# Latent inputs of batches 1 to 7 made inside the perceiver, context worked first

## The chip, the cores and the metric

One NeuronCore of one Trainium2 chip runs the whole program. The metric is the device time of one execution in microseconds (us); lower is better. TensorE is the matrix engine, VectorE, ScalarE and GpSimd are the elementwise engines, and SP (SyncE) mostly issues DMAs.

## The reference, cut to what matters

Two layers over x (8 batches, 512 tokens, D = 512) with a context of 77 rows a batch. The part that matters here is the hand-over from layer 0 to the cross attention of layer 1:

```
out0 = einsum(alpha, slot_values) @ wo + bo          # layer 0's slot feed-forward
x2   = x1 + out0                                     # residual
xn   = layernorm(x2);  z  = layernorm(xn) * ln_l_g + ln_l_b     # the latents of layer 1
cn   = layernorm(ctx); zc = cn * ln_x_g + ln_x_b
q    = z @ Wq                                        # 16 heads of 64
k, v = concat(z, zc) @ Wkv                           # 512 + 77 keys
o    = softmax(q k' / 8, masked) v                   # per batch and head
```

The two nested norms of x2 are worked as one (the variance v becomes v (1 + eps) + eps squared). Behind it come Wout, a norm and a routed expert feed-forward on x2. Every product with a weight is made of a high and a low float32r part (three products for one), to keep float32 accuracy.

## The kernel before, in words

The program is a row of stages, each a block of instructions with its own buffers, queues and semaphores, and a barrier between two stages: `build_layer0` (0 to 676 us), `build_slots` (to 828), `build_latents` (to 1000), `build_perceiver` (to about 2485) and `build_experts`. Each engine's program is written out by hand in order, and every dependence is an explicit wait on a semaphore mark.

**Slots** (lines 999 to 1322) makes vo_s, the slots' values already multiplied by wo. It also splits the weights Wq and Wkv through three staging areas of WihT; when the last is cut, SP loads x1 of batches 0 and 1 into two of these areas (line 1100), where the next stage finds them.

**Latents** (lines 1325 to 1651) runs over the 8 batches. For each, TensorE makes the read-out alpha @ vo (`read_out`, line 1478, 4 tiles of 128 tokens; a last row of ones with bo gives the bias); VectorE adds x1 (line 1608), measures it (1611, 1616), GpSimd makes the root (1466, 1468), VectorE normalises (1631), TensorE transposes (1486), ScalarE scales by the gains (1556) and casts the high part (1560), VectorE takes the low part (1641), and x2 and both parts of z go to HBM. Beside them the stage works the context rows once: statistics (1594), normalising (1623), transposes (1495, 1500), scaling and cast (1537 to 1546), low part (1638). Then, one head pair of keys per batch (`keys`) and ten value units of 128 rows x 512 columns spread over the batches (`values`), it makes the context's keys and values for all heads and stores them (Kc_s, Vc_s). Keys and values share banks 6 and 7, and the value tile in SBUF is single, so the cast of a tile waits for the store of the tile before. The context rows themselves are loaded by SP at this stage's start (line 1428) behind the first small loads, ahead of the gains.

**Perceiver** (lines 1661 to 2131) runs over 128 heads (8 batches x 16) in 512 steps of one tile of 128 queries, four steps to a head and eight to a pair of heads. In step n TensorE issues the scores of step n + 1 into one of two score banks, then, by n modulo 4: the last two products with the values of the head before last (0), transposes of two of the five key blocks of probabilities (1), transposes of two more and two products (2), the last transposes and a product (3). Once per pair it also makes the query (n = 1 modulo 8) and the key (3) of the next pair, and in steps 6 and 7 a value unit. VectorE takes the minimum of the negated scores of step n (line 2113), the reciprocals (2109) and all low parts (2066, 2081, 2098); ScalarE the exponentials (2034), all high parts (2005) and the output's cast (2053); GpSimd multiplies the probabilities (1880) and takes the output's low part (1874). Queries, keys, values and transposes share three banks: `claim` gives a unit the bank that was released longest ago and waits until VectorE has read the unit that lay there before. SP, in one program per pair, loads the context's keys and values, copies halves, loads z at each batch's last pair, stores the output two pairs late, and clears a part of the experts' buffer.

Of the kernel before, what the change touches and what calls it, by code (L numbers as in the profile page):

```python
# [20 lines left out]
P = 128  # L21
# [90 lines left out]
def f32(ap):  # L112

    return ap.bitcast(F32)
# [884 lines left out]
def build_slots(nc, orders, a, si_s, vo_s, Wq, Wkv, Wout_s, gh_s, WihT, x1_s):  # L999
# [11 lines left out]
    with ExitStack() as ctx:  # L1011
# [71 lines left out]
        def _(sp):  # L1083
# [15 lines left out]
            for n in range(2):  # L1099
                sp.dma_start(stage(n), x1_s[n:n + 1].rearrange("b (t p) d -> p (b t) d", p=P)).then_inc(x1_in, 16)  # L1100
# [5 lines left out]
            sp.wait_ge(x1_in, 32)  # L1106
# [218 lines left out]
def build_latents(nc, orders, a, x1_s, alphaT_s, vo_s, x2_s, z_s, Kc_s, Vc_s, Wkv, ahead):  # L1325
# [13 lines left out]
    RING = 3  # L1339

    with ExitStack() as ctx:
# [18 lines left out]
        rows_c = [f32(z_hi[1][:, k, :]) for k in range(KT - 1)] + [f32(z_lo[1][0:LAST, 0, :])]  # L1360
# [3 lines left out]
        setup, small, ones_row, cx_in = sem("setup"), sem("small"), sem("ones_row"), sem("cx_in")  # L1364
        x1_in = [sem(f"x1_in{r}") for r in range(RING)]
# [10 lines left out]
        batch = lambda b: 0 <= b < B  # L1376
        v_items = [(k, h) for k in range(KT) for h in range(2)]
        v_of = lambda b: v_items[b * len(v_items) // B:(b + 1) * len(v_items) // B]
        place = {"x2": lambda b, t: (b * NT + t) % 3, "zT": lambda b, c: 3 + (b * C + c) % 3, "cT": lambda c: 3 + c % 3,
# [20 lines left out]
        def _(sp):  # L1400
            flat = a["ctx_1024"].rearrange("b s d -> (b s) d")
            def load_small(b):
                m = b % 2
                if b >= 2:
                    sp.wait_ge(*pe_s.after("x2", b - 2, NT - 1))
# [3 lines left out]
            def load_x(b):  # L1409
                r = b % RING  # L1410
                if b >= RING:
                    sp.wait_ge(x2_out[r], 16 * (b // RING))
                    sp.wait_ge(*dve_s.after("xn", b - RING, NT - 1))
                sp.dma_start(X[r], x1_s[b:b + 1].rearrange("b (t p) d -> p (b t) d", p=P)).then_inc(x1_in[r], 16)
# [12 lines left out]
            for k in range(KT):  # L1427
                sp.dma_start(rows_c[k], flat[k * P:k * P + rows_of(k), :]).then_inc(cx_in, 16)
            for dst, src in smalls:
                sp.dma_start(dst, src).then_inc(small, 16)  # L1430
            load_small(1)
            load_x(2)
            for b in range(B):
                sp.wait_ge(*dve_s.after("free", "x2", b, NT - 1))
                sp.dma_start(x2_s[b:b + 1].rearrange("b (t p) d -> p (b t) d", p=P), X[b % RING]).then_inc(x2_out[b % RING], 16)
                if batch(b + 2):
                    load_small(b + 2)
                if batch(b - 1):
                    for q, h in [i for i in v_of(b - 1) if i[1]]:
                        values_out(q)  # L1440
                    keys_out(b - 1)
                if batch(b + 2) and b > 0:
                    load_x(b + 2)
# [1462 lines left out]
```

## Time and profile before

| what | us |
| --- | --- |
| median of 3 runs (2917.95 to 2927.77) | 2923.05 |
| the profiled execution | 2921.61 |
| its span | 2919.8 |
| TensorE busy in it | 2646.1 (91%) |
| VectorE, ScalarE, GpSimd busy | 2023.6, 1517.6, 1522.0 |
| mean granted TensorE clock | 0.953 of full |

The profile is of one execution; its times are microseconds from the span's start. In the names, la_ is a buffer of the latents stage, pa_ of the perceiver, sl_ of slots, ex_ of the experts. "128x512 fp32r<-128x512 f32 x4" says what an instruction writes, from what, and how many stand in the group; PEld is the weight load, SPq and ACTq are DMA issues on those engines' queues; "[0.31 <-DVE pa_PTl L2066]" says how long the engine was idle before the instruction and what ended that. A granted clock of 1.00 is 2.4 GHz, one of 0.50 is 1.2 GHz. A row of the view of stretches gives start:end, length, and the busy time (with the number of instructions) of TensorE, its weight loads, VectorE, ScalarE and GpSimd, then the granted clock, the share of the DMA engines and GB/s.

### The profile page before, as it was taken

How to read it: one execution, taken by the hardware profiler on the slowest of the kernel's cores; microseconds unless marked ns; L12 is line 12 of the kernel's file. 1: busy time of each engine (PE TensorE's matmuls, PEld its weight loads, DVE VectorE, ACT ScalarE, POOL GpSimd, SP SyncE). 2: the span in 40 equal slices, each digit the busy share in tenths (PEclk: the TensorE clock that was granted, in tenths of full speed). 3: DMA queues.
4: the chain of work that ended last, by engine and by line, in shares of the span. 5: the costliest groups of instructions: out<-in, count | busy, mean ns of one | idle time of the engine just before them, and what ended most of it. 6: DMA issues, size and time to landing. Idle time of an engine off the chain costs nothing. (4 is left out here: it accounts for less than half of the span.)

```text
span 2919.8 us, 41005 instructions
## 1 busy us (share of the span) xinstructions
PE 2646.1 (91%) x14566; PEld 2188.7 (75%) x14566; DVE 2023.6 (69%) x4005; ACT 1517.6 (52%) x2897; POOL 1522.0 (52%) x1149
## 2 busy tenths in 40 slices
PE   6699999986778699999999999999999998799698
PEld 5577777763436588888888888888888887677476
DVE  3677777742546377777777777777777777577666
ACT  2234334331213277777777777777777777111175
POOL 2355544320000166666666666666666666465555
PEclk9899999998878899999999999999999999899899
DMA  5212222133348633334333343233433314668475
GB/s 188 56 54 56 56 57 57 41 96 128 139 145 312 228 74 80 106 83 115 81 77 109 80 118 81 75 111 76 122 80 77 109 51 136 210 238 288 157 275 187
DMA packets 212526, 351.15 MB, mean 120 GB/s; under 512 B 75839, under 2 KB 82370, under 8 KB 204631
## 3 DMA queue, kind: packets, MB, share of 16 engines
q1 hardware_dynamic: 193539, 284.89, 32.8%
q0 software_dynamic: 11680, 45.02, 4.2%
q10 hardware_dynamic: 7104, 18.61, 1.6%
q8 instruction: 117, 1.92, 0.3%
q14 instruction: 86, 0.70, 0.1%
HBM read 172.47 MB, written 156.64 MB: 113 GB/s over the span
## 5 line engine op out<-in xcount | busy, mean ns | idle before, releaser
L1880 POOL TENSOR_SCALAR pa_Pr<-pa_Pr,pa_rs 128x590 f32<-128x590 f32 x512 | 902.4, 1769 | 485.1 <-DVE pa_rs L2109 484.9
L2113 DVE TENSOR_REDUCE pa_least<-pa_S 128x1 f32<-128x590 f32 x512 | 390.7, 763 | 230.0 <-PE pa_S L1944 227.9
L2034 ACT ACTIVATE pa_Pr<-pa_S,pa_least 128x590 f32<-128x590 f32 x512 | 385.5, 753 | 99.4 <-DVE pa_least L2113 96.0
L2066 DVE TENSOR_TENSOR pa_PTl<-pa_W,pa_PTh 128x512 fp32r<-128x512 f32 (+1 forms) x640 | 421.2, 684 | 20.5 <-ACT pa_PTh L2005 16.4
L2005 ACT ACTIVATE pa_PTh<-pa_W 128x512 fp32r<-128x512 f32 (+1 forms) x640 | 367.0, 596 | 58.4 <-PE pa_W L1955 47.1
L1955 PE MATMUL pa_W<-pa_ident,pa_Pr 128*128 128x128 f32 (+1 forms) x2560 | 369.7, 275 | 0.6
L1955 PEld LDWEIGHTS pa_W<-pa_ident,pa_Pr 128*128 128x128 f32 (+1 forms) x2560 | 302.4, 142 | 30.0 <-POOL pa_Pr L1880 2.8
L1971 PE MATMUL pa_O<-pa_PTh,pa_V 128*128 128x512 f32 (+1 forms) x640 | 289.2, 452 | 18.6 <-DVE pa_PTl L2066 14.4
L1972 PE MATMUL pa_O<-pa_PTl,pa_V 128*128 128x512 f32 (+1 forms) x640 | 253.4, 396 | 0.0
L1942 PE MATMUL pa_S<-pa_U,pa_Qh 128*128 128x296 f32 (+1 forms) x1024 | 228.9, 305 | 7.5 <-ACT pa_Pr L2034 0.5
L1942 PEld LDWEIGHTS pa_S<-pa_U,pa_Qh 128*128 128x128 f32 x1024 | 183.2, 188 | 55.5 <-ACT pa_Pr L2034 21.3
L1944 PE MATMUL pa_S<-pa_Um,pa_Ql 128*128 128x296 f32 (+1 forms) x1024 | 222.7, 299 | 0.0
L514 POOL TENSOR_TENSOR l_E<-l_E,l_rs 128x1232 f32<-128x1232 f32 x32 | 81.1, 2533 | 204.0 <-DVE l_rs L916 204.0
L1944 PEld LDWEIGHTS pa_S<-pa_Um,pa_Ql 128*128 128x128 f32 x1024 | 166.4, 189 | 0.0
L1971 PEld LDWEIGHTS pa_O<-pa_PTh,pa_V 128*128 128x128 f32 (+1 forms) x640 | 121.4, 190 | 45.0 <-DVE pa_PTl L2066 36.1
L119 PE MATMUL pa_W<-Wkv_hi,pa_z_hi 128*128 128x256 f32 x512 | 144.9, 283 | 0.0
L120 PE MATMUL pa_W<-Wkv_lo,pa_z_hi 128*128 128x256 f32 x512 | 144.2, 282 | 0.0
L121 PE MATMUL pa_W<-Wkv_hi,pa_z_lo 128*128 128x256 f32 x512 | 143.9, 281 | 0.0
L1972 PEld LDWEIGHTS pa_O<-pa_PTl,pa_V 128*128 128x128 f32 (+1 forms) x640 | 123.0, 192 | 5.2
L2560 ACT ACTIVATE ex_xT_hi<-ex_bank 128x512 fp32r<-128x512 f32 x92 | 53.4, 599 | 141.3 <-PE ex_bank L2456 134.9
L119 PE MATMUL pa_W<-pa_z_hi,Wq_hi 128*128 128x512 f32 x256 | 106.9, 418 | 17.8 <-POOL pa_Ql L1871 17.8
L2005 ACT ACTIVATE pa_U<-pa_W 64x512 fp32r<-64x512 f32 x128 | 75.8, 592 | 89.7 <-PE pa_W L121 88.1
(503 smaller groups left out, 6545.6 us busy)
## 6 DMA issues: line engine op xcount, KB each, us to landing
xs_s<-pa_Ql SPq DMA_DIRECT2D x57, 576.0 KB
pa_Um<-pa_U SPq DMA_DIRECT2D x128, 147.5 KB
pa_Qh<-pa_Qh SPq DMA_DIRECT2D x128, 128.0 KB
o_s<-pa_O_hi SPq DMA_DIRECT2D x64, 256.0 KB, 2.0
o_s<-pa_O_lo SPq DMA_DIRECT2D x64, 256.0 KB, 2.3
Wkv_hi<-o_s SPq DMA_DIRECT2D x8, 2048.0 KB, 11.3
Wkv_lo<-o_s SPq DMA_DIRECT2D x8, 2048.0 KB, 17.0
l_xa<-x SPq DMA_DIRECT2D x8, 1024.0 KB, 6.5
```

The lines of the kernel that those rows point to most:

```text
L119: pe.matmul(out, a[0], b[0], start=first, stop=False)
L120: pe.matmul(out, a[0], b[1], start=False, stop=False)
L1880: pool.tensor_scalar(p, p, rs[:, g % 2, t:t + 1], None, ALU.mult).then_inc(*pool_s.mark("probs", n))
L1942: pe.matmul(out[:, a0:a1], qh, U[p % 2][x][:, a0:a1], start=True, stop=False)
L1944: m = pe.matmul(out[:, a0:a1], ql, Um[p % 2][x][:, a0:a1], start=False, stop=True)
L1955: m = pe.transpose(bank_of[u][0:KEYS[c], t * P:(t + 1) * P], Pr[g % 2][:, t, c * P:c * P + KEYS[c]], ident[:, :])
L1971: pe.matmul(Oc[:, :], v, PTh[0:n, r, :], start=(c == 0), stop=False)
L1972: pe.matmul(Oc[:, :], v, PTl[0:n, r, :], start=False, stop=(c == NC - 1)).then_inc(*pe_s.mark("PV", g, c))
L2005: act.activation(out, src, ACT.Copy, scale=scale).then_inc(*act_s.mark("hi", *name))
L2034: act.activation(Pr[g % 2][:, t, :], scored[n % 2], ACT.Exp, scale=-1.0, bias=least[:, g % 2, t:t + 1], accum_out=rs[:, g % 2, t:t + 1]).t ...
L2066: dve.tensor_tensor(out, src, f32(hi_ap), ALU.subtract).then_inc(*dve_s.mark(*name))
L2113: dve.tensor_reduce(least[:, g % 2, t:t + 1], scored[n % 2], AX, ALU.min).then_inc(*dve_s.mark("least", n))
```

## The change

The latents stage keeps only batch 0 of the latents (FIRST = 1). Context rows come with the slots stage's last loads (in the place of batch 1's x1) and are worked first: TensorE transposes them ahead of the read-out, VectorE takes their low parts ahead of batch 0's adding. The eight key pairs and ten value units follow in a loop of their own, with batch 0's transposes, casts and low parts behind the first pair.

The latents of batches 1 to 7 are made in the perceiver, one tile of 128 tokens at a time, 28 tiles, in the steps of the batch before. Tile t of batch b starts in step n0 = 64 (b - 1) + 12 t, and its parts are put at fixed distances: inputs fetched at n0 - 2 (ScalarE's DMA queue), ones row n0 - 1 (VectorE), read-out n0 (TensorE), add and measure n0 + 1 (VectorE), root n0 + 2 (GpSimd) and x2 stored (ScalarE's queue), normalise n0 + 3 (VectorE), transpose n0 + 4 (TensorE), scale n0 + 5 (VectorE, where it was ScalarE), cast n0 + 6 (ScalarE), first store n0 + 7 and low part (VectorE), second store n0 + 8. To make room in SBUF, the output's sum and its low part share one buffer: ScalarE's first write of a pair's output waits for the store of the pair before, the output's cast on ScalarE and low part on GpSimd come one step earlier (t = 1 in place of 2).

```diff
@@ build_slots, SP
-            for n in range(2):
-                sp.dma_start(stage(n), x1_s[n:n + 1].rearrange("b (t p) d -> p (b t) d", p=P)).then_inc(x1_in, 16)
+            sp.dma_start(stage(0), x1_s[0:1].rearrange("b (t p) d -> p (b t) d", p=P)).then_inc(x1_in, 16)
+            sp.dma_start(stage(1)[:, 0:whole, :], flat[0:whole * P, :].rearrange("(k p) d -> p k d", p=P)).then_inc(x1_in, 16)
+            sp.dma_start(stage(2)[0:flat.shape[0] - whole * P, 0, :], flat[whole * P:, :]).then_inc(x1_in, 16)
@@ build_latents
-    RING = 3
+    RING, FIRST = 1, 1
@@ TensorE
             pe.wait_ge(setup, 4)
+            context()
             pe.wait_ge(ones_row, 2)
             pe.wait_ge(small, 16 * len(smalls))
-            read_out(0)
-            context()
-            for b in range(B):
-                if batch(b + 1):
-                    read_out(b + 1)
-                transposed(b)
+            for b in range(FIRST):
+                read_out(b)
+            for b in range(PAIRS):
                 keys(b)
                 for k, h in v_of(b):
                     values(k, h)
+                if batch(b):
+                    transposed(b)
@@ build_perceiver
+        APART = 3 * NT
+        tiles = [(b, t) for b in range(1, B) for t in range(NT)]
+        begins = {STEPS // B * (b - 1) + APART * t: i for i, (b, t) in enumerate(tiles)}
+        tile_at = lambda n, late: begins.get(n - late)
@@ SP
             def load(b):
+                if b:
+                    sp.wait_ge(z_out, 32 * NT * b)
@@ GpSimd
-                if t == 2 and g >= 3 and g % 2 == 1:
+                if t == 1 and g >= 3 and g % 2 == 1:
                     low_part((g - 3) // 2)
+                i = tile_at(n, 2)
+                if i is not None:
+                    pool.wait_ge(*dve_s.after("x2 var", i))
+                    pool.tensor_scalar(lve, lmv[:, 1:2], 1.0 + EPS, EPS * EPS, ALU.mult, ALU.add).then_inc(*pool_s.mark("x2 ve", i))
+                    pool.wait_ge(*pool_s.after("x2 ve", i))
+                    pool.tensor_tensor(lrstd, lve, minus_half, ALU.pow).then_inc(*pool_s.mark("x2 rstd", i))
@@ TensorE
+            def residual(i):
+                u = ("x2", i)
+                claim(u)
+                pe.wait_ge(x_in, 32 * (i + 1))
+                pe.wait_ge(vo_in, 16 * (i // NT + 2))
+                pe.wait_ge(*dve_s.after("ones", i))
+                pe.matmul(bank_of[u][:, :], alphas[0:NS + 1, :], vo[:, :], start=True, stop=True).then_inc(*pe_s.mark(*u))
+                release(u)
+            def latent(i):
+                u = ("zT", i)
+                claim(u)
+                pe.wait_ge(*dve_s.after("xn", i))
+                for c in range(C):
+                    m = pe.transpose(bank_of[u][:, c * P:(c + 1) * P], ln[:, c * P:(c + 1) * P], ident[:, :])
+                m.then_inc(*pe_s.mark(*u))
+                release(u)
@@ ScalarE
+            def fetch(i):
+                ...
+                    act.wait_ge(z_out, 32 * i)
+                act.dma_start(lx[:, :], x1_s[b, t * P:(t + 1) * P, :]).then_inc(x_in, 16)
+                act.dma_start(alphas[0:NS, :], alphaT_s[b][:, t * P:(t + 1) * P]).then_inc(x_in, 16)
+                ...
                     if x == 0 and p > 0:
-                        act.wait_ge(*pool_s.after("O lo", p - 1))
+                        act.wait_ge(o_out, 32 * p)
@@ VectorE
+            def add_and_measure(i):
+                dve.wait_ge(*pe_s.after("x2", i))
+                dve.tensor_tensor(lx[:, :], bank_of["x2", i][:, :], lx[:, :], ALU.add).then_inc(*dve_s.mark("read", "x2", i))
+                ...
+            def normalised(i):
+                dve.wait_ge(*pool_s.after("x2 rstd", i))
+                dve.wait_ge(*dve_s.after("x2 var", i))
+                dve.tensor_scalar(ln[:, :], lx[:, :], lmv[:, 0:1], lrstd, ALU.subtract, ALU.mult).then_inc(*dve_s.mark("xn", i))
+            def scaled(i):
+                ...
+                for c in range(C):
+                    m = dve.tensor_scalar(ln[:, c * P:(c + 1) * P], bank_of["zT", i][:, c * P:(c + 1) * P], gain[0][:, c:c + 1], gain[1][:, c:c + 1],
+                                          ALU.mult, ALU.add)
+                m.then_inc(*dve_s.mark("read", "zT", i))
+            def latent_low(i):
+                dve.wait_ge(*act_s.after("z hi", i))
+                dve.tensor_tensor(ln[:, :], ln[:, :], lx[:, :], ALU.subtract).then_inc(*dve_s.mark("z lo", i))
@@
+                for late, work in ((-1, ones), (1, add_and_measure), (3, normalised), (5, scaled), (7, latent_low)):
+                    if tile_at(n, late) is not None:
+                        work(tile_at(n, late))
```

## Rows read from the trace of the kernel before

**Rows 1.** View of stretches: the latents stage, and the perceiver's steps.
```profile
828.40:999.70 171.30, 124.57 (x524) 90.96 (x524) 100.09 (x207) 59.45 (x102) 14.05 (x22) 0.82 0.72 263
...
1018.80:2467.00 1448.20, 1427.38 (x8856) 1254.68 (x8855) 1122.38 (x2097) 1051.21 (x2157) 975.33 (x572) 1.00 0.34 93
```

**Rows 2.** Timeline of VectorE at the latents' start: start us, us, instruction.
```profile
828.72 1.02 DVE L1589 MEMSET la_aT<- 1x512 f32 x2 [2.55 <-PEq L1011]
836.86 2.47 DVE L1594 BATCH_NORM_STATS2 la_cstats<-la_z_hi 128x6 f32<-128x512 f32 x4 [7.11 <-DMA la_z_lo<-ctx]
...
839.96 0.45 DVE L1598 BATCH_NORM_AGGREGATE la_cmv<-la_cstats 128x2 f32<-128x6 f32 x5
...
848.42 1.88 DVE L1623 TENSOR_SCALAR la_z_hi<-la_z_hi,la_cmv,la_crstd 128x512 f32<-128x512 f32 x4
```

**Rows 3.** Timeline of TensorE, the same stretch.
```profile
848.99 4.41 PE L1495 MATMUL la_bank<-la_ident,la_z_hi 128*128 128x128 f32 x16 [4.01 <-DVE la_z_hi L1623]
...
853.73 3.62 PE L1478 MATMUL la_bank<-la_vo,la_aT 65*128 65x512 f32 x8
857.18 1.48 PE L1486 MATMUL la_bank<-la_ident,la_xn 128*128 128x128 f32 x12
...
861.60 0.41 PE L119 MATMUL la_bank<-la_zc_hi,Wkv_hi 128*128 128x308 f32 x1 [2.13 <-DVE la_zc_lo L1638]
```

**Rows 4.** Timeline of GpSimd, the same stretch.
```profile
849.07 1.27 POOL L1468 TENSOR_TENSOR la_rstd<-la_ve,la_minus_half 128x4 f32<-128x4 f32 x1
```

**Rows 5.** Timeline of ScalarE: cast of the context, a DMA issue.
```profile
856.79 1.31 ACT L1546 ACTIVATE la_zc_hi<-la_K_lo 128x616 fp32r<-128x616 f32 x2
...
966.80 0.33 ACTq L1562 DMA_DIRECT2D z_s<-la_z_hi  x1
```

**Rows 6.** Timeline of TensorE: two value units, first and last of 24.
```profile
983.84 0.48 PE L119 MATMUL la_bank<-Wkv_hi,la_zc_hi 128*104 128x512 f32 x1 [0.73 <-DVE la_K_lo L1646]
...
989.25 0.39 PE L121 MATMUL la_bank<-Wkv_hi,la_zc_lo 128*104 128x512 f32 x1
```

**Rows 7.** Timeline of TensorE in one head pair of the perceiver.
```profile
1314.87 0.47 PE L119 MATMUL pa_W<-pa_z_hi,Wq_hi 128*128 128x512 f32 x1
...
1330.04 0.66 PE L1955 MATMUL pa_W<-pa_ident,pa_Pr 128*128 128x128 f32 x4
...
1335.81 0.40 PE L1971 MATMUL pa_O<-pa_PTh,pa_V 77*128 77x512 f32 x1
```

**Rows 8.** Timeline of VectorE and GpSimd in the slots stage.
```profile
774.40 0.89 DVE L1237 COPY sl_AT<-sl_bank 128x128 f32<-128x128 f32 x4
...
778.62 0.69 DVE L1300 TENSOR_TENSOR sl_y<-sl_bank,sl_bv_bc 128x512 f32<-128x512 f32 x1 [2.20 <-PE sl_bank L1172]
...
780.08 0.18 DVE L1304 BATCH_NORM_AGGREGATE sl_mv<-sl_stats 128x2 f32<-128x6 f32 x1
...
782.83 1.19 DVE L1251 TENSOR_TENSOR Wkv_lo<-WihT,Wkv_hi 128x1024 fp32r<-128x1024 f32 x1
...
783.01 1.10 POOL L1117 TENSOR_SCALAR sl_rstd<-sl_mv 128x1 f32<-128x1 f32 x1 [0.88 <-DVE sl_mv L1304]
...
788.32 0.44 POOL L1117 TENSOR_SCALAR sl_rstd<-sl_mv 128x1 f32<-128x1 f32 x1 [0.90 <-DVE sl_mv L1304]
```

**Rows 9.** Timeline of VectorE in the same head pair as rows 7.
```profile
1327.69 0.69 DVE L2098 TENSOR_TENSOR pa_O_sum<-pa_O,pa_O_sum 64x512 f32<-64x512 f32 x1
...
1329.31 1.28 DVE L2066 TENSOR_TENSOR pa_PTl<-pa_W,pa_PTh 128x512 fp32r<-128x512 f32 x2
...
1333.76 0.68 DVE L2066 TENSOR_TENSOR pa_PTl<-pa_W,pa_PTh 77x512 fp32r<-77x512 f32 x1
```

**Rows 10.** Timeline of GpSimd in that pair.
```profile
1328.68 1.77 POOL L1880 TENSOR_SCALAR pa_Pr<-pa_Pr,pa_rs 128x590 f32<-128x590 f32 x1 [3.10 <-DVE pa_rs L2109]
...
1332.48 1.28 POOL L1874 TENSOR_TENSOR pa_O_lo<-pa_O_sum,pa_O_hi 128x512 fp32r<-128x512 f32 x1
```

**Rows 11.** DMA issues on the page; the last number is us from issue to landing.
```profile
o_s<-pa_O_lo SPq DMA_DIRECT2D x64, 256.0 KB, 2.3
```

More of the change, by code:

```diff
@@ L1566, in low_out @@
                 act.dma_start(z_s[1][b], f32(z_lo[b % 2][:, :, :])).then_inc(z_out[b % 2], 16)
-            for b in range(B):
-                latents(b)
+            for b in range(PAIRS):
                 for h in range(2):
@@ L1582, in _ @@
                     act.activation(hi, src, ACT.Copy).then_inc(*act_s.mark("hi", "V", k, h))
-            for m in range(2):
-                act.wait_ge(z_out[m], 32 * (B // 2))
+                if batch(b):
+                    latents(b)
+                if batch(b - 1):
+                    low_out(b - 1)
+            act.wait_ge(z_out[0], 32)
         @block.vector
@@ L1632, in _, with low @@
                                       ALU.subtract, ALU.mult).then_inc(*dve_s.mark("xn", b, t))
[L1633 to L1638 removed]
+            def low(b):
+                m = b % 2
                 for c in range(C):
@@ L1641, in _ @@
                     dve.tensor_tensor(z_lo[m][:, c, :], full[m][:, c, :], f32(z_hi[m][:, c, :]), ALU.subtract).then_inc(*dve_s.mark("lo", b, c))
+            add_and_measure(0)
+            normalised(0)
+            for b in range(PAIRS):
                 for h in range(2):
@@ L2000, in _ @@
                     value(q, j)
+                if tile_at(n, 0) is not None:
+                    residual(tile_at(n, 0))
+                if tile_at(n, 4) is not None:
+                    latent(tile_at(n, 4))
         @block.scalar
@@ L2057, in _ @@
                     probabilities(g - 1, 4)
+                if tile_at(n, -2) is not None:
+                    fetch(tile_at(n, -2))
+                if tile_at(n, 2) is not None:
+                    keep(tile_at(n, 2))
+                i = tile_at(n, 6)
+                if i is not None:
+                    act.wait_ge(x2_out, 16 * (i + 1))
+                    act.wait_ge(*dve_s.after("read", "zT", i))
+                    act.activation(l_hi, ln[:, :], ACT.Copy).then_inc(*act_s.mark("z hi", i))
+                i = tile_at(n, 7)
+                if i is not None:
+                    act.wait_ge(*act_s.after("z hi", i))
+                    latent_out(0, i)
+                i = tile_at(n, 8)
+                if i is not None:
+                    act.wait_ge(*dve_s.after("z lo", i))
+                    latent_out(1, i)
                 if STEPS <= n < STEPS + 4:
```

151 lines of the change are left out of this document (81 added, 70 removed).

## The prediction

> **What bounds the kernel now.** I read the view of stretches first. The latents stage (828.4 to 999.7) takes 171.3 us, in which TensorE is busy 124.6 us at a granted clock of 0.82; the 1448.2 us of the perceiver's steps show TensorE busy 1427.4 us at clock 1.00, VectorE 1122.4, ScalarE 1051.2, GpSimd 975.3 [rows 1]. So the first stage is a chain of waits, and the second is TensorE's: 64 head pairs of 22.6 us, eight steps each. Work moved from one to the other leaves a stage where it partly hid and enters one where every TensorE microsecond counts. Then I read the timelines of the latents' start and of one head pair (1313 to 1337).
>
> **The latents stage: its start.** Before, VectorE's context statistics wait for the context rows until 836.86, though its own work would let them start at 829.8 (two memsets end at 829.74) [rows 2]. In the new stage they start there. Statistics and aggregates take 3.55 us (836.86 to 840.41), GpSimd's root 1.8 us (what it took for batch 0, from the aggregates' end at 848.51 to 850.34) [rows 2, 4]; then the normalised rows. TensorE's first transpose comes 0.57 us after their start (848.42 to 848.99) [rows 2, 3]: 829.8 + 3.55 + 1.8 + 0.6 = 835.7. Transposes and four read-out products took TensorE 8.4 us (848.99 to 857.35), so it would be at 844.1 [rows 3]. ScalarE's cast of the context ends 9.1 us after the first transpose (848.99 to 858.10) [rows 3, 5]: 844.8. Keys start about 844, 17.6 us sooner than at 861.60 [rows 3]. The new loads in the slots stage (1.2 MB of context in place of 1 MB of x1) go out behind the last weight cut, on SP, some 30 us before that stage ends: nothing.
>
> **Its body.** 24 value products of 512 columns take 5.65 us (983.84 to the last start, 989.25, and one spacing), so 2.83 us per value unit; key pairs of 24 products with 308 columns 3.4 us, by columns [rows 6]. Eight key pairs and ten value units: 55.5 us. They share banks 6 and 7, and a bank is free only when ScalarE and VectorE have read it, some 1.4 us. In the new order VectorE does batch 0's adding, measuring and normalising (5.6 for four of the 1.64 below less its gaps, 1.8 for the root, 1.9 for four normalisings [rows 8, 4, 2]) after the context's low parts (845.6) and ahead of the first key's low part, so value (0,0) starts about 855.6 instead of 847.5. It ends 858.4, the latents' transposes about 861.5, key pair 1 at 865; value (0,1) waits until 866.7 for a bank, behind the latents' casts on ScalarE and low parts on VectorE. Left are nine value units and six key pairs, 45.9 us, five bank waits of 1.2 to 1.5 us, and one of 5 us where value (2,0) follows value (1,1) directly and ScalarE needs the store of the whole first tile landed: 11.6 us. With 4 us for stretches at the lower clock TensorE ends at 928; the end took 10.2 us (989.5 to 999.7), now 9.7 as the keys' stores go first. New end 937.7: **62 us less**, with bounds of 52 (clock 0.82 all through, a second store wait) and 66 (no low clock).
>
> **The perceiver: plain costs.** For each of 28 tiles TensorE gets a read-out product, 0.86 us (four in 3.45 us from 853.73 to 857.18, the next group's first row), and four transposes, 0.40 us (twelve took 1.48 with the last one's drain) [rows 3]: 1.26 us, 35 in all. VectorE gets add, statistics and aggregate, 1.64 us (778.62 to 780.26) [rows 8]; normalising 0.5 (four in 1.88, 848.42) [rows 2]; scaling four blocks, 0.9 (the nearest row copies four 128x128 blocks in 0.89) to 1.1, taken 1.0 [rows 8]; a low part 0.65 (two in 1.28) [rows 9]; a memset, under 0.5 (two of 1x512 took 1.02) [rows 2]: 4 to 4.3 us, some 115 in all, against 326 us idle [rows 1]. ScalarE gets a cast (0.6; two of 616 columns took 1.31) and five or six DMA issues of 0.33 us, 0.43 with the gap [rows 5]; GpSimd 0.9 to 1.8 us. None of these three becomes the bound as a sum. They matter where a bank is claimed: TensorE has three banks, takes the longest released, and waits for VectorE's last read of it.
>
> **The perceiver: waits.** I replay one pair with the new work in its places; steps are counted modulo 8. In the trace VectorE runs without a gap from the scores' minimum of step 5 through the key's low parts and the output sum (from 1327.69, end 1328.38) to the first low part of the probabilities (1329.31 to 1329.95), and TensorE's third transpose group, which needs that bank, starts at 1330.04: in steps 5 and 6 any VectorE time delays TensorE one for one [rows 9, 7].
> Tiles 0 and 2 (start in step 0): the product costs 0.86. VectorE's 1.64 fall in idle time behind the query's 2.8 us. In step 4 come the transposes; in step 5 VectorE scales behind the output sum, and the value unit of step 6 draws exactly this bank: TensorE moves by the scaling, 1.0, in place of 0.4. Sum 1.9 us.
> Tiles 1 and 3 (start in step 4): the product's 0.86 is inside VectorE's 1.64, which sits in the gapless run: 1.6 us. GpSimd then gets its factor 1.7 us late, at 1330.2, does the probabilities (1.77), the pair's low part (1.28), which the change puts one step earlier, the next probabilities (1.77), and only then the variance and root, 0.9 [rows 10]: ready at 1336.1. VectorE reaches the normalising at 1334.5 and waits 1.6. The fifth low part (1333.76 to 1334.44) ends at 1338.4; the product on it (1335.81) starts there, 2.6 late [rows 9, 7]. Then 0.4 for the transposes, and the query draws their bank: scaled at 1342.2. The query starts 4.6 us late against 1314.87 plus the pair. Sum 4.6.
> 14 tiles of each: **91 us**. At the start tile 0's inputs are issued on ScalarE about 1018.5 and land behind other loads; TensorE would wait for them some 2.5 us. The earlier reuse of the output sum, which now waits for its store, costs nothing while GpSimd ends it in step 6 and stores land in 2.3 us [rows 11]; without that, up to 1 us on ScalarE per pair. SP gains a wait ahead of each latents load, in front of a pair's store and its blanks; the last part of a batch goes out seven steps before, so it holds nothing up. ScalarE's fetch waits for the store of the tile before, with the exponentials behind it; that store goes out two steps (5 us) sooner, and 256 KB landed in 2.3 us [rows 11]: nothing either.
>
> **A rule against the trace.** One GpSimd scalar operation on 128x1 took 1.10 us (783.01) while VectorE ran a subtraction of two SBUF operands (782.83 to 784.02) [rows 8]; the same operation took 0.44 us at 788.32, with no such subtraction beside it [rows 8]. The Trainium skill, "SBUF — State Buffer", section "Who interferes with whom", says that such a VectorE instruction and a GpSimd one that reads SBUF exclude each other, the later waiting for the whole of the earlier. By that rule each tile's new low part would wait for GpSimd's 1.77 us. The sum above leaves this out; it is part of rival D.
>
> **Sum.** The profiled execution took 2921.61 us, its span 2919.8, the median of three 2923.05. 2921.6 - 62 + 2.5 + 91 = 2953.1, so **2953 us** (the median is 1.4 above its base).
>
> **Rivals.**
> A, the forecast: bank waits and the late root add to the moved work. For it: the gapless run [rows 9]. Against: one pair was replayed, and the bank order by hand. 0.43.
> B, the moved work is hidden but for TensorE's own time: 2921.6 - 62 + 2.5 + 35 = 2897, up to 2905 with short waits. For it: three engines have over 300 us idle each [rows 1]. Against: the gapless run sits in the very steps used. This is the case on the other side; it decides for faster if waits per tile stay under 0.55 us, (62 - 2.5 - 35 - 9) / 28. 0.24.
> C, bank waits as in A, but the root is not late (tiles 1 and 3 cost 2.8): 14 x (1.9 + 2.8) = 66, 2928. 0.18.
> D, A plus inputs of a tile that land after TensorE asks for them (256 KB took 2.3 us alone [rows 11], the fetch goes out 4 us ahead into SP's store and blanks, 0 to 1.5 us on 28 tiles) or VectorE waiting for GpSimd, 0 to 0.8 us a tile: up to 42 + 22 us on top, 2970 to 3015. 0.12.
> E, the latents stage is bound by the bank pair and its stores throughout, and saves only 50 with C's costs: 2940. 0.03.
>
> **Numbers.** A measurement of this kernel can tell about 0.3% (9 us) from no change. Faster by more: B, 0.24. Within: most of C, 0.17. Slower: A, D, E and the rest of C, 0.59. The range, 2898 to 2990, takes in B at its middle and D's lower half.
>
> **What would show it.** The latents stage 105 to 120 us long, its first statistics near 829.8, keys near 844; 4.6 us lost on odd tiles and 1.9 on even ones; steps from 1448 to some 1540 us; VectorE's normalising waiting on GpSimd's root; TensorE waiting on the scaling. The forecast is wrong if a batch with tiles is less than 8 us longer than before (then B or C), or if the latents stage saves less than 50.

## The result, and the profile after

The changed kernel takes 2962.87 us (median of 4 runs, 2962.23 to 2965.04) against 2923.64 (4 runs of the kernel before on the same chip): ratio 1.0137, 95% interval 1.0119 to 1.0155. It is slower. The profiled execution took 2963.48 us, its span is 2961.7.

First the two stretches of [rows 1] in the kernel after: the latents stage, and the steps of the perceiver.

```profile
833.00:939.00 106.00, 72.16 (x356) 59.06 (x356) 33.57 (x67) 24.37 (x46) 3.46 (x10) 0.87 0.34 128
958.10:2512.50 1554.40, 1476.23 (x9016) 1273.32 (x9016) 1222.33 (x2373) 1069.01 (x2182) 995.13 (x628) 0.99 0.40 107
```

The latents stage took 171.3 us and takes 106; the steps took 1448.2 and take 1554.4, with TensorE busy for 1476.2 of them, VectorE for 1222.3. TensorE's idle time in this stretch rose from 21 us to 78, of which 13.5 is one stall near its end (below).

For the accounting both traces are divided at instructions that both have: VectorE's first memset of the latents stage, the first exponential of step 0, that of step 504 (eight steps from the end), that of step 511, the end. The kernel before, then after:

```profile
828.70:1020.30 191.60, 137.45 (x596) 102.39 (x597) 104.83 (x215) 62.42 (x107) 21.19 (x42) 0.81 0.70 253
1020.30:2454.00 1433.70, 1413.88 (x8772) 1243.48 (x8771) 1110.26 (x2073) 1040.66 (x2134) 962.79 (x565) 1.00 0.34 90
2454.00:2471.10 17.10, 13.60 (x84) 10.85 (x82) 12.25 (x26) 11.95 (x26) 14.99 (x10) 1.00 0.82 304
2471.10:2919.80 448.70, 382.61 (x1818) 304.24 (x1818) 292.13 (x653) 140.51 (x225) 242.97 (x350) 0.90 0.63 222
```

```profile
833.30:960.50 127.20, 85.90 (x435) 71.38 (x436) 38.48 (x76) 27.34 (x51) 10.38 (x29) 0.85 0.38 135
960.50:2487.30 1526.80, 1462.26 (x8933) 1261.28 (x8932) 1211.79 (x2351) 1059.87 (x2162) 984.66 (x622) 1.00 0.39 105
2487.30:2515.60 28.30, 14.23 (x82) 11.81 (x81) 12.47 (x25) 12.03 (x26) 13.57 (x9) 0.76 0.49 183
2515.60:2961.70 446.10, 379.19 (x1822) 300.01 (x1820) 293.67 (x653) 139.98 (x225) 244.31 (x350) 0.91 0.63 223
```

The second number of a row is its length. Differences: 64.4 us less up to step 0; 93.1 more in steps 0 to 504; **11.2 more in the last eight steps**; 2.6 less behind them; and 4.6 us more ahead of the first mark, in code that is the same but for the loads (over the traces of this study that mark falls anywhere from 826.2 to 834.3, so experiments are read by stretch). Together 41.9, the difference of the spans. In steps 0 to 504 TensorE's busy time rose by 48.4 us and its idle time by 44.7.

The start of the latents on TensorE, against [rows 3]:

```profile
840.32 4.17 PE L1476 MATMUL la_bank<-la_ident,WihT 128*128 128x128 f32 x16 [10.32 <-DVE WihT L1595]
...
844.68 3.62 PE L1459 MATMUL la_bank<-la_vo,la_aT 65*128 65x512 f32 x8
848.25 0.41 PE L119 MATMUL la_bank<-la_zc_hi,Wkv_hi 128*128 128x308 f32 x1
...
859.30 0.79 PE L119 MATMUL la_bank<-Wkv_hi,la_zc_hi 128*128 128x512 f32 x1 [6.53 <-DVE la_K_lo L1621]
```

Keys begin 15.0 us after the memset at 833.3, where they took 32.9 (forecast 844 - 828.7 = 15.3). Then a hole of 6.5 us opens ahead of the first value unit: VectorE reaches the key's low part only behind batch 0's adding, measuring and normalising. That was forecast (first value unit 26.9 us after the memset, measured 26.0).

What the steps wait for (engine, line, what released it: us in total, times, longest):

```profile
PE pa_W L119 <- DVE pa_xn_next L2197: 26.0, 28, 1.0
...
DVE pa_xn_next L2191 <- POOL pa_norm L1884: 22.0, 14, 1.6
ACT pa_O_sum L2029 <- DMA o_s<-pa_O_sum: 20.8, 6, 13.9
...
PE pa_S L1944 <- ACT pa_Pr L2084: 13.6, 2, 13.5
...
PE pa_W L1982 <- DMA pa_vo<-vo_s: 5.0, 4, 2.4
```

L2191 is the normalising: it waits for GpSimd's root 14 times, up to 1.6 us, just the odd tiles. L2197 is the scaling: TensorE waits for its bank 28 times. The longest wait for value vectors, 2.4 us, is the first tile's (2.5 was forecast). L2029 is ScalarE's first copy into a pair's output sum: one of its waits is 13.9 us, and TensorE's scores stand still for 13.5 with it. The clock granted in that stretch is 0.76 instead of 1.00.

One odd tile (its step 0 at 1193), VectorE and then GpSimd, against [rows 9, 10]:

```profile
1200.27 0.69 DVE L2134 TENSOR_TENSOR pa_PTl<-pa_W,pa_PTh 128x512 fp32r<-128x512 f32 x1
1201.18 0.69 DVE L2134 TENSOR_TENSOR pa_PTl<-pa_W,pa_PTh 128x512 fp32r<-128x512 f32 x1 [0.21 <-ACT pa_PTh L2029]
1203.44 0.55 DVE L2191 TENSOR_SCALAR pa_xn_next<-pa_x_next,pa_norm 128x512 f32<-128x512 f32 x1 [1.57 <-POOL pa_norm L1884]
```

```profile
1199.45 1.27 POOL L1870 TENSOR_TENSOR pa_O_sum<-pa_O_sum,pa_O_hi 128x512 f32<-128x512 f32 x1
1200.71 1.77 POOL L1876 TENSOR_SCALAR pa_Pr<-pa_Pr,pa_rs 128x590 f32<-128x590 f32 x1
1202.56 0.19 POOL L1882 TENSOR_SCALAR pa_norm<-pa_norm 128x1 f32<-128x1 f32 x1
1202.83 0.57 POOL L1884 TENSOR_TENSOR pa_norm<-pa_norm 128x1 f32<-128x1 f32 x1
```

GpSimd does probabilities, the pair's low part, probabilities, and only then the root, which ends at 1203.40; VectorE had been free since 1201.87. From the starts of the exponentials, twelve steps from a tile's step 0 against the same steps before: an odd tile costs 3.86 us (mean of 14, 3.6 to 4.8), an even one 2.53 (mean of 13), and the very first 6.3. A batch's last 16 steps cost nothing.

### The profile page after: what moved, and what is told of

The parts are those of the page before. It is cut to its first block and busy times, and to the rows that moved or that the text cites. A ratio compares the mean times of both kernels' runs of the same rounds, so it can differ in the third digit from the quotient of the medians.

```text
span 2961.7 us, 41403 instructions
## 1 busy us (share of the span) xinstructions
PE 2645.0 (89%) x14566; PEld 2174.4 (73%) x14566; DVE 2060.3 (70%) x4145; ACT 1501.8 (51%) x2869; POOL 1533.0 (52%) x1192
## 5 line engine op out<-in xcount | busy, mean ns | idle before, releaser
L2029 ACT ACTIVATE pa_PTh<-pa_W 128x512 fp32r<-128x512 f32 (+1 forms) x640 | 368.8, 596 | 88.4 <-PE pa_W L1957 78.7
L1957 PEld LDWEIGHTS pa_W<-pa_ident,pa_Pr 128*128 128x128 f32 (+1 forms) x2560 | 302.7, 142 | 40.1 <-DVE pa_PTl L2134 10.9
L1944 PE MATMUL pa_S<-pa_U,pa_Qh 128*128 128x296 f32 (+1 forms) x1024 | 242.4, 318 | 17.3 <-ACT pa_Pr L2084 13.6
L2209 DVE RECIPROCAL pa_rs<-pa_rs 128x1 f32<-128x1 f32 x512 | 80.8, 158 | 64.9 <-ACT pa_Pr L2084 62.4
```

The lines of the kernel that those rows point to most:

```text
L1944: pe.matmul(out[:, a0:a1], qh, U[p % 2][x][:, a0:a1], start=True, stop=False)
L1957: m = pe.transpose(bank_of[u][0:KEYS[c], t * P:(t + 1) * P], Pr[g % 2][:, t, c * P:c * P + KEYS[c]], ident[:, :])
L2029: act.activation(out, src, ACT.Copy, scale=scale).then_inc(*act_s.mark("hi", *name))
```

## The experiments

Totals are medians; a ratio is to runs of the kernel before on the same chip. "Steps" means steps 0 to 504 of the profiled execution, 1433.7 us before and 1526.8 in the changed kernel. How far one such reading can be trusted: four kernels that leave these steps without tiles (share_only, ctx_first, ctx_keys, norm_ahead) show 1433.2 to 1434.2, but store_first, whose instructions are the changed kernel's up to step 504, shows 1532.8, 6.0 more. With tiles, a difference of a few us in the steps is read from the cost of the single tiles.

### 1. What a tile costs, engine by engine

**TensorE alone** (te_only). Latents for all eight batches ahead of the perceiver (that stage is experiment 4's first), the changed kernel's shared output buffer with its earlier cast and low part, and of the tiles only this:

```diff
 def residual(i): / def latent(i):
-    pe.wait_ge(x_in, ...); pe.wait_ge(vo_in, ...); pe.wait_ge(*dve_s.after("ones", i))
-    pe.matmul(bank_of[u], alphas[0:NS + 1, :], vo)
+    pe.matmul(bank_of[u], ident[0:NS + 1, :], vo)
-    m = pe.transpose(bank_of[u][...], ln[...], ident)
+    m = pe.transpose(bank_of[u][...], ident, ident)
+def freed(kind, i):                      # VectorE
+    dve.wait_ge(*pe_s.after(kind, i))
+    dve.tensor_copy(lve, bank_of[kind, i][:, 0:1])
```

> Latents stage as in the run with the context first, with all eight batches; in the perceiver's steps 28 tiles of TensorE's work alone: a read-out product and four transposes of constant tiles, each bank freed by a copy of one column by VectorE; no fetch, no sum, no statistics, no root, no scaling, no store. The output is complete. Theory (TensorE is busy 1426 of 1446 us, so its own work costs its full time): 28 x 1.26 = 35 us more than the run with the context first alone, steps about 1481 us. Rival (part of it falls into waits that TensorE has anyway, or the third bank decides): 15 to 25 us, or over 45 us.

Measured 2960.18 us, ratio 1.0136 (1.0114 to 1.0158). The two rows are steps 0 to 504 and the last eight:

```profile
1019.80:2479.50 1459.70, 1441.74 (x8939) 1261.89 (x8938) 1115.19 (x2128) 1044.51 (x2135) 961.96 (x566) 1.00 0.34 88
2479.50:2508.20 28.70, 14.48 (x82) 12.06 (x81) 12.41 (x25) 11.97 (x26) 13.49 (x9) 0.76 0.48 180
```

Steps 1459.7 us, 25.7 more than the 1434.0 of the run with the context first: 0.92 us a tile, not 1.26 (two one-column copies on VectorE included). That is 9 us under the theory and just above the rival's 15 to 25. TensorE is busy 27.6 us more (1441.7 against 1414.1), a fifth less than the 35 forecast. The clock is not the reason: the rows that gave 1.26 stand in a stretch (853.7 to 857.3) with a granted clock of 1.00, and a read-out product takes 0.59 us there as here. Where the rest went is not shown. The last eight steps took 28.7 us though no tile falls into them: the tiles do not make this stall, and the shared buffer is in this kernel too (experiment 3).

**VectorE's and ScalarE's part on top** (te_dve, te_act). The same with VectorE's operations of a tile on constant data, without root, rounding, fetch or store; and with ScalarE's fetches, rounding and stores on data that nobody reads:

```diff
-for late, work in ((1, lambda i: freed("x2", i)), (5, lambda i: freed("zT", i))):
+for late, work in ((-1, ones), (1, add_and_measure), (3, normalised), (5, scaled), (7, latent_low)):
```

> The run with TensorE's tile work alone, and with it VectorE's operations of a tile (memset, sum, statistics, aggregation, normalising, four scalings, low part) on constant tiles: no root on GpSimd, no rounding, no fetch and no store on ScalarE. Output complete. Steps 0 to 504 took 1459.7 us with TensorE's work alone and 1526.8 us in the changed kernel; 10.5 of these 67 us were the root's order. Theory (VectorE's 4.6 us a tile, 28 times, lie in the loop of scores, minimum and exponential that sets a step): 40 to 57 us more, 1500 to 1517 us. Rival (ScalarE's queue with its five issues of DMAs and one rounding a tile is what is left): at most 20 us more, under 1480 us.

> The run with TensorE's tile work alone, and with it ScalarE's part of a tile: the fetches, the store of the sum, the rounding and the two stores of the halves, with data that nobody reads, into rows of the batch before that are no longer needed. Output complete. Theory (VectorE holds most of the 67 us): 5 to 15 us over the 1459.7 us of steps 0 to 504. Rival (ScalarE's issues, 0.33 to 0.54 us each, stand between two exponentials): 35 us or more, 1495 us or more.

Measured 3010.98 us, ratio 1.0301 (1.0278 to 1.0324), and 2971.55 us, ratio 1.0178 (1.0153 to 1.0203). The latents stage of these two is not the changed kernel's, so only the steps count:

```profile
1028.70:2535.00 1506.30, 1456.07 (x8939) 1262.79 (x8938) 1217.66 (x2351) 1047.51 (x2135) 964.08 (x566) 1.00 0.33 86
```

```profile
1023.80:2490.60 1466.80, 1445.48 (x8933) 1263.16 (x8932) 1114.89 (x2128) 1056.27 (x2163) 963.50 (x566) 1.00 0.41 109
```

VectorE adds 46.6 us, ScalarE 7.1. Both came as expected. Half of the 7.1 is the very first tile, whose inputs land late (5.0 us in that run against 1.5 without the fetch). With TensorE's 25.7 and the 10.6 of the root (next) that makes 90.0 of the 93.1 us. By tile, te_dve costs 2.39 us an even tile and 2.69 an odd one, against 2.53 and 3.86 in the changed kernel: even tiles are TensorE's and VectorE's work and little else, odd ones have the root on top. VectorE does 102.5 us more work there than with TensorE's part alone (1217.7 against 1115.2): a little under half of it shows in the time.

### 2. The waits inside a tile

**The root ahead of the probabilities** (root_early).

```diff
 for n in range(STEPS):
     g, t = divmod(n, NT)
+    (the four lines that wait for "x2 var" and make the root)
     pool.wait_ge(*dve_s.after("rsum", n))
     ...
-    (the same four lines)
```

> The changed kernel, but GpSimd makes a tile's root ahead of that step's probabilities instead of behind them. Theory (VectorE's 1.57 us wait on the root, 14 times in tiles that start in step 4 mod 8, is on the path): odd tiles fall from 3.85 to about 2.4 us, 14 x 1.4 = 20 us, total about 2943 us. Rival (VectorE's wait was hidden, and what lengthens odd tiles is the order of banks): the wait is gone from the trace but the total stays within 3 us of 2963. Third way (probabilities late by .76 us hold up the transposes): some 5 to 10 us only.

Measured 2955.67 us, ratio 1.0114 (1.0092 to 1.0137). Steps 1516.2, 10.6 less; odd tiles from 3.86 to 2.87 us, even ones nearly unchanged (2.53 and 2.64). The theory, 20 us, missed by half; the total, 7 us lower, lies where the third way had it, though its reason is not shown. The wait is gone, but part of its place is taken by a longer normalising (durations ns min/median/max):

```profile
L2191 DVE TENSOR_SCALAR pa_xn_next<-pa_x_next,pa_norm x28: 536/718/911, 973.9 to 2248.1; 128x512 f32<-128x512 f32 x28
L2203 DVE TENSOR_TENSOR pa_xn_next<-pa_xn_next,pa_x_next x28: 680/682/684, 984.3 to 2261.3; 128x512 f32<-128x512 f32 x28
```

```profile
1201.22 0.57 POOL L1879 TENSOR_TENSOR pa_norm<-pa_norm 128x1 f32<-128x1 f32 x1
1201.78 5.26 POOL L1882 TENSOR_SCALAR pa_Pr<-pa_Pr,pa_rs 128x590 f32<-128x590 f32 x3
```

```profile
1201.92 0.89 DVE L2191 TENSOR_SCALAR pa_xn_next<-pa_x_next,pa_norm 128x512 f32<-128x512 f32 x1
```

In odd tiles it now runs beside GpSimd's probabilities and takes 0.89 us instead of 0.55. 1.57 - 0.35 would be 1.2 us a tile; 1.0 came. The other 0.2 is not explained.

**The scaling in two operations** (scale_two).

```diff
-for c in range(C):
-    m = dve.tensor_scalar(ln[block c], bank[block c], gain[0][:, c:c + 1], gain[1][:, c:c + 1], ALU.mult, ALU.add)
-m.then_inc("read zT")
+dve.tensor_tensor(rows(ln), rows(bank), wide[0], ALU.mult).then_inc("read zT")
+dve.tensor_tensor(rows(ln), rows(ln), wide[1], ALU.add).then_inc("z full")
```

ScalarE's cast then waits for "z full".

> The changed kernel, but the scaling is one product with the broadcast gain, which frees the bank, and one sum with the broadcast offset in SBUF, about 0.69 and 0.65 us in place of four operations of 0.40. Theory (TensorE's 26 us of waits for the scaling, 28 times, are on the path and fall by about 0.8 us each): 15 to 22 us less, 2941 to 2948 us. Rival (VectorE's time as such is what a tile costs, and that falls by 0.2 us a tile): 2957 to 2960 us.

Measured 2959.55 us, ratio 1.0122 (1.0096 to 1.0148); steps 1519.5, 7.3 less. From 1060 to 2440 us, weight loads (PEld) and matmuls of TensorE:

```profile
PEld pa_W L119 <- DVE pa_xn_next L2198: 12.9, 25, 0.6
...
PE pa_W L1957 <- DVE pa_PTl L2134: 12.1, 25, 0.6
```

In the changed kernel the first of these was 29.8 us, 25 times; so the wait for the scaled bank fell by more than half, 17 us. But the second was 7.5 us, 13 times: transposes of the probabilities now wait more often for VectorE's next pieces. A bank freed earlier moves part of the wait to what VectorE does after it. The total is the rival's (2957 to 2960), the theory's 15 to 22 us did not come. But the rival's reason is not shown either: by it every tile falls by 0.2 us, and what fell is the odd tiles alone, from 3.86 to 3.21 (mean of 14), while the even ones stayed (2.53 and 2.63).

**All tiles in one phase** (phase_even).

```diff
-begins = {STEPS // B * (b - 1) + APART * t: i ...}
+begins = {STEPS // B * (b - 1) + (APART * t if b == 1 else 4 * NT * t - 2 * NT): i ...}
```

> The changed kernel with the tiles of batches 2 to 7 started in steps -8, 8, 24 and 40 of the batch before instead of 0, 12, 24 and 36, so that all of them start in step 0 mod 8 (batch 1's stay). Theory (a tile that starts in step 4 mod 8 costs 3.85 us, one in step 0 mod 8 costs 2.45 us): 12 tiles x 1.4 = 17 us less, 2944 to 2949 us. Rival (the tile at -8 meets the four value units at the end of a batch, three banks for all of them, and loses the gain): 2955 us or more.

Measured 2977.72 us, ratio 1.0179 (1.0153 to 1.0205): 15 us slower than the changed kernel, steps 1537.7, 10.9 more. A batch's first 48 steps fell by 3 to 6 us; about 2.5 of that is the tile that moved out of them, the rest is near the theory's 1.4 each for the tiles at 8 and 40. But the tile at -8 cost 5 to 8 us in a batch's last eight steps. From 1060 to 2440 us:

```profile
PEld pa_W L1982 <- issue: 16.1, 10, 4.3
...
PE pa_W L1982 <- DMA pa_vo<-vo_s: 12.3, 6, 3.8
```

Its read-out product waited for the batch's value vectors, up to 3.8 us, in the steps where four value units share three banks. The rival was right, and named only half of it: I had not priced the load.

### 3. The stall in step 504

**The shared output buffer alone** (share_only), on the kernel before:

```diff
-O = sb("O_sum", [P, T])
-Os = pair("O", [P, T])
+Os = sb("O_hi", [P, T], F32R), sb("O_sum", [P, T])
+O = Os[1]
...
-act.wait_ge(*pool_s.after("O lo", p - 1))
+act.wait_ge(o_out, 32 * p)
```

> The kernel before with one part of the change alone: the low part of a pair's output is written over the sum, so ScalarE's first copy of a pair waits for the store of the pair before, and the rounding and the low part come a step earlier. Theory (this part alone makes the stall of 13 us in step 504, of which 3 to 6 us come back after the last scores): 7 to 11 us over before, all of it in the last eight steps. Rival (the stall needs the late steps of the changed kernel): no difference to before.

Measured 2937.03 us, ratio 1.0042 (1.0021 to 1.0063).

```profile
1022.40:2455.60 1433.20, 1413.04 (x8771) 1243.39 (x8771) 1109.24 (x2072) 1042.58 (x2134) 962.55 (x566) 1.00 0.34 90
2455.60:2485.50 29.90, 14.72 (x83) 12.33 (x82) 12.53 (x26) 12.06 (x27) 13.64 (x9) 0.77 0.47 177
```

The steps take what they took before (1433.2), the last eight 29.9 instead of 17.1: 12.8 us, by this part of the change alone. Behind them the experts' first product comes 1.2 us sooner after step 511 than before. The forecast priced it at nothing.

**The store first** (store_first), on the changed kernel:

```diff
-if p == PAIRS - 1:
-    ahead()
 if p >= 2:
     store(p - 2)
+if p == PAIRS - 1:
+    ahead()
```

> The changed kernel, but in the last pair SyncE stores pair 61's output before it issues the loads ahead for the experts. Theory (the 13.9 us stall of ScalarE in step 504 is the store queued behind the 1 MB weight load, and the shared output buffer made it bind): the stall goes, the last eight steps lose 11 us, of which some 3 to 5 us come back after the last scores because the loads start two steps later; total 2952 to 2959 us. Rival (the weight load is needed just as early): the same wait turns up at its split in steps 512 to 515 and the total stays at 2963.

Measured 2956.82 us, ratio 1.0111 (1.0085 to 1.0138). SyncE's issues in the changed kernel, and then with the store first:

```profile
2480.55 0.53 SPq L1780 DMA_DIRECT2D Wq_lo<-Wout_s  x1
...
2481.86 3.68 SPq L1783 DMA_DIRECT2D Wkv_lo<-o_s  x1
2485.59 6.39 SPq L1775 DMA_DIRECT2D o_s<-pa_O_hi  x1
2492.02 0.55 SPq L1775 DMA_DIRECT2D o_s<-pa_O_sum  x1
```

```profile
2489.31 0.33 SPq L1775 DMA_DIRECT2D o_s<-pa_O_hi  x1
...
2490.22 0.41 SPq L1780 DMA_DIRECT2D Wq_lo<-Wout_s  x1
...
2491.39 5.71 SPq L1783 DMA_DIRECT2D Wkv_lo<-o_s  x1
```

```profile
958.30:2491.10 1532.80, 1465.51 (x8932) 1263.75 (x8931) 1212.23 (x2351) 1059.19 (x2162) 984.47 (x622) 1.00 0.39 104
2491.10:2505.40 14.30, 13.10 (x82) 10.64 (x81) 12.37 (x25) 11.89 (x26) 13.53 (x9) 1.00 0.99 350
2505.40:2959.20 453.80, 382.93 (x1822) 304.43 (x1820) 289.46 (x653) 140.45 (x225) 243.37 (x350) 0.90 0.63 222
```

In the changed kernel the store of pair 61 is issued behind 6 MB of loads for the experts (three of 2 MB; the theory named one of 1 MB), the issue alone takes 6.4 us, and ScalarE's copy that waits for it starts at 2502.08. With the store first the last eight steps take 14.3 us, 14.0 less. The stretch behind them is 7.7 us longer. Of these, 5.8 lie between step 511 and the experts' first product (26.4 us against 20.6; 25.8 in the run with three edits): the loads start later. The rest cannot be put down to the edit, as the experts' part, the same code everywhere, takes 424 to 433 us over the traces of this study. So some 8 us are gained. The stall is as the theory had it, a little more of it than expected comes back, and the 6.0 us more in the steps, which the edit does not touch, are not its doing: in one tile, near 1425, the store of the output and the tile's inputs land 6 us after their issue instead of 4, and the steps there lose 3.9 us.

**Three edits together** (three): root_early, scale_two, store_first.

> The changed kernel with three edits together: GpSimd's root ahead of the probabilities, the scaling in two whole operations, and SyncE's store ahead of the loads for the experts. Theory (the gains of 10.5, 7.3 and 6 us lie in different steps and add up): 24 us less, 2936 to 2943 us, still 15 us over the kernel before. Rival (root and scaling follow each other in one tile, so one gain hides the other): 2945 us or more.

Measured 2933.57 us, ratio 1.0037 (1.0023 to 1.0052).

```profile
959.90:2464.90 1505.00, 1461.92 (x8933) 1262.64 (x8932) 1217.34 (x2295) 1058.13 (x2163) 984.14 (x622) 1.00 0.40 105
```

Steps 1505.0, 21.8 less where the single edits gave 10.6 and 7.3; odd tiles 2.2 us. The gains add up; the 4 us beyond them are within what such steps differ by. It is 29 us better than the change as made, and still not better than the kernel before.

### 4. The other half of the change by itself

If the tiles cost 93 us in the perceiver, what did they cost where they were? **The context first, all eight batches in the latents stage, the perceiver of before** (ctx_first):

```diff
-read_out(0)
 context()
+read_out(0)
 for b in range(B):
-    if batch(b + 1): read_out(b + 1)
-    transposed(b)
     keys(b)
     for k, h in v_of(b): values(k, h)
+    if batch(b + 1): read_out(b + 1)
+    transposed(b)
```

with the context's rows loaded in the slots stage as the change does, and the other engines in that order.

> The perceiver of before and all eight batches' latents in the latents stage, but the context rows come in the slots stage and are normalised, transposed and split first, and each batch's keys and values stand ahead of its transposes. Theory (the latents stage owes its gain to two things, 18 us of earlier keys and about 48 us of batches 1 to 7 taken out): stage 171 to about 153 us, the steps unchanged at 1446, total about 2905 us (2900 to 2911). Rival (TensorE's idle time before the keys was only moved, since the batches' own chain over VectorE sets the stage): stage still 168 or more, total 2920 or more.

Measured 2926.66 us, ratio 1.0013 (1.0 to 1.0027): a miss. Keys began 18.8 us after the memset instead of 32.9, but the first exponential came after 193.4 us instead of 191.6. TensorE in this stage:

```profile
PE la_bank L119 <- DVE la_K_lo L1644: 24.7, 8, 3.6
```

and in the kernel before:

```profile
PE la_bank L119 <- DVE la_K_lo L1646: 8.4, 7, 1.8
```

24.7 us, eight times, for the split of a key that VectorE reached behind the next batch's work; before it was 8.4. The early keys were lost to the order of the loop.

**The loop of before, keys one batch earlier** (ctx_keys):

```diff
+context(); read_out(0); keys(0)
 for b in range(B):
     if batch(b + 1): read_out(b + 1)
     transposed(b)
-    keys(b)
+    if batch(b + 1): keys(b + 1)
     for k, h in v_of(b): values(k, h)
```

The other engines follow that order, VectorE takes the context's low parts between batch 0's sums and its statistics, and batch 0's last sum gets another bank. (Lines with + or - are against the kernel before.)

> The perceiver of before and all eight batches' latents in the latents stage in the loop order of before; the context rows come in the slots stage and are worked first, and each pair's keys stand one batch earlier (the first ahead of batch 0's transposes). Theory (in the run with the context first the keys began 10 us earlier, and 12 us were lost again because VectorE reached the splits of keys and values late; with the loop order of before that loss goes): keys from about 850, the stage from 171 to 155 to 160 us, the steps unchanged, 11 to 16 us less than before, 2906 to 2912 us. Rival (VectorE's 80 us and ScalarE's 49 us of eight batches in one chain set the stage's length whatever the keys do): 168 us or more, within 4 us of before.

Measured **2912.90 us**, ratio 0.9963 (0.9949 to 0.9976): just past the upper end of the theory.

**And the next normalising ahead of the values' split** (norm_ahead), on that kernel, VectorE:

```diff
+normalised(0)
 for b in range(B):
-    normalised(b)
     ...
     split_keys(b + 1)
+    normalised(b + 1)
     (split of the values)
```

> The run with keys one batch earlier, and VectorE normalises the next batch's rows (1.9 us) ahead of the split of the values, where it stood idle 3.4 us a batch waiting for ScalarE, instead of behind it. Theory (TensorE's 12.5 us of waits for the fourth bank of the sums, 7 times, come from VectorE's sums standing behind the normalising): sums 1.9 us earlier in 6 or 7 batches, the stage 8 to 12 us shorter than the 180.6 us from its first instruction to the first exponential, total 2901 to 2906 us. Rival (the values' split, later by part of the 1.9 us, holds a bank for the next keys as long as the sums did): within 3 us of 2912.9.

Measured **2900.65 us**, ratio 0.9909 (0.9888 to 0.9930). From the memset to the first exponential, for the two kernels, and what TensorE waited for in them:

```profile
828.50:1009.10 180.60, 132.47 (x597) 100.84 (x598) 104.79 (x215) 62.91 (x107) 20.34 (x42) 0.85 0.74 267
```

```profile
829.40:999.20 169.80, 126.95 (x597) 95.89 (x598) 105.27 (x215) 60.85 (x107) 21.81 (x42) 0.86 0.78 284
```

```profile
PE la_bank L1479 <- DVE WihT L1615: 12.5, 7, 5.3
```

```profile
PE la_bank L1479 <- DVE WihT L1615: 5.9, 2, 4.9
```

191.6 us before, 180.6, 169.8; the steps stay at 1434. Beside the shorter wait for the sums, that for the split of a key rose from 8.3 to 11.4 us. This last kernel is 24 us faster than before (2924.64 on the same chip) and 62 faster than the change as made.

So, from the memset to the first exponential, all eight batches in the better order take 169.8 - 127.2 = 42.6 us more than batch 0 alone, and 64.4 more with the late context in the order of before. The seven batches cost 93 us in the perceiver's steps, 71 with the repairs.

## Why the prediction was right, and where it was off

- **The sign and the sum.** 2953 was forecast, 2962.9 measured. Its three large terms: latents 62 less (64.4 measured); perceiver's steps 93.5 more with the first tile (93.1 measured); nothing else (8.6 measured). That 93.5 met 93.1 is partly luck: its parts were off both ways, as below, and the same steps took 99.1 more in store_first.
- **The step that failed** is "the earlier reuse of the output sum ... costs nothing while GpSimd ends it in step 6 and stores land in 2.3 us". 2.3 us is the median of 64 stores [rows 11]. One of them is issued behind the experts' loads, landed late already before (the rounding waited 3.0 us for it), and the change moved the first waiter six steps forward. share_only shows 12.8 us in the last eight steps, store_first takes the stall away again. With that term the forecast would have stood at 2962 to 2964.
- **Even tiles 1.9, odd 4.6** were forecast; 2.5 and 3.9 came. The mechanisms were there: the root's wait was 1.57 to 1.58 us in the places predicted, the scaling's bank was waited for 28 times. The sizes: four scalings take 1.35 us, not 1.0 (their nearest row was a copy, without the two factors); TensorE's own part is 0.92, not 1.26; removing the root's wait gives 1.0 an odd tile, not 1.8 (4.6 - 2.8), of which 0.35 is the slower normalising that comes in its place. The errors cancel over 28 tiles: the sum was better than its parts, and that is luck.
- **ScalarE's part at nothing** was nearly right: 7.1 us in 28 tiles.
- **Rival B** (moved work hidden but for TensorE's own) fell with te_only: that state would be 25.7 us of steps. VectorE's 46.6 come on top: of 102.5 us that it works more, a little under half shows. Idle time summed over a stage (326 us) said little; the place in the loop said it.
- **Rival C** is nearly what root_early ran: its odd tiles cost 2.87, as C had it (2.8). Its total, 2955.67, is not C's 2928: even tiles cost 2.64, the first 6.3, and the last eight steps' stall is in it.
- **Rival D**'s late inputs: 5.0 us in 4 waits for value vectors, 2.4 of them at the start, and in store_first 3.9 us in one place; small. Its other part, VectorE excluded by GpSimd, did not come: in the 13 places where a tile's low part overlaps GpSimd's 1.77 us it takes 0.68 us as elsewhere.

What the forecast did not ask is what the gain could be had for without the move. The stage it called "a chain of waits" gives 22 us to an earlier load and two changes of order, with all its work in place.

## What to carry to other kernels

Before work is moved out of a stage that is bound by waits, look whether reordering removes the waits: here the move saved 64 us there, and 22 of them were to be had with all the work in place. In a loop where the engines hand on to each other every step, an engine's idle time does not cover new work: nearly all of TensorE's and half of VectorE's showed in the time. When a buffer is reused earlier, price the latest of its transfers, not the median: find in the trace the one that is queued behind something large. Read from the timeline of a step, not from a summed idle time, whether an engine is idle where the new operation will stand.

## What the runs showed of the hardware

- **VectorE and GpSimd on SBUF.** VectorE's normalising (one SBUF tile of 128x512, two factors by partition) takes 0.54 us with GpSimd idle, and 0.89 to 0.91 (root_early) or 0.97 to 0.99 (te_dve) beside GpSimd's scaling of the probabilities, which keeps its 1.77 to 1.79 us. A subtraction of two SBUF tiles takes 0.68 us with GpSimd idle and 0.68 in 13 places where it overlaps the same GpSimd operation (in scale_two it lies wholly inside it). The Trainium skill, "SBUF — State Buffer", section "Who interferes with whom", says that the two-input form contends with GpSimd's reads, and that in the two-port modes whoever comes second is blocked for the whole of the other's instruction. For these two pairs the measurement differs: the subtraction is not held, and the normalising ran on, slower, and ended 0.7 us before the GpSimd operation did (no run shows in which mode it runs). But other places of the kernel before do show the first half of the rule:

```profile
L2689 DVE TENSOR_TENSOR ex_Wt<-ex_g,ex_Wt x16: 679/685/1779, 2531.2 to 2739.7; 128x512 fp32r<-128x512 f32 x16
```

```profile
L1468 POOL TENSOR_TENSOR la_rstd<-la_ve,la_minus_half x8: 1006/1139/1536, 849.1 to 965.3; 128x4 f32<-128x4 f32 x8
```

  The subtraction of the first row took 1.77 to 1.78 us in the three places where GpSimd's sum of two 128x512 tiles had begun some 0.5 us before it, and that sum took 1.73 to 1.75 instead of about 1.29 where the subtraction had begun first. The root of the second row took 1.54 us both times that it began 0.02 us into a low part on VectorE, 1.01 where none had begun before it. The 1.10 us of [rows 8] stands three times in the slots stage, each time ending 0.1 us after VectorE's subtraction. So the forecast read that row rightly; what it priced, GpSimd's scaling holding up a low part, is the case where nothing is held. The 28 variances of the tiles took 0.19 us each, but none ran beside a VectorE instruction with two SBUF tiles, so they say nothing on it.
- **The issue of a DMA blocks its queue.** SyncE's issue of a 256 KB store took 6.39 us behind three loads of 2 MB, against 0.33 for most (in the kernel before 3.38, behind the same loads).
- **The clock of TensorE** was granted at 0.76 over the last eight steps where the stall fell and TensorE stood still for 13.5 us, at 1.00 over the same steps before and in store_first, without the stall.
